# Norm, quantisation and transposes of x rearranged in a fused attention and gate kernel

## The chip, the cores and the metric

The kernel runs on one core of a Trainium2 chip. The metric is device time in microseconds of one execution. Engines: TensorE (PE, matmuls), VectorE (DVE), ScalarE (ACT), GpSimd (POOL) and SyncE (SP, which issues all DMA transfers here).

## The reference

For each of 8 batches of 512 tokens with 512 features, x is layer-normed to xn; `s` is a differential attention over xn, `g` a gate from xn and a weight that are both rounded to MXFP4; the result is `x + s * g`.

```python
qkv = hidden_states @ Wqkv_w.T + Wqkv_b            # 16 q heads, 8 k heads, 4 v of 256
p1 = attn_map(q[:, :, :, 0], k[:, :, :, 0])        # causal softmax
p2 = attn_map(q[:, :, :, 1], k[:, :, :, 1])
p = p1 - lam * p2
o = jnp.einsum('bhqk,bkhe->bqhe', p, v)
rms = jax.lax.rsqrt(jnp.mean(o * o, axis=-1, keepdims=True) + EPS)
o = o * rms * subln_w * (1.0 - LAMBDA_INIT)
s = o.reshape(B, S, H * D) @ out_w.T + out_b
# gate: blocks of 32 share a power-of-two scale; elements are rounded to e2m1
g = silu(quant_dequant_mxfp4(xn) @ quant_dequant_mxfp4(weight).T + bias)
x = x + s * g
```

## The kernel before

Every operand of a large matmul is kept as two float16 parts, high and low, and each product is three matmuls (lines 456 to 458: high by high, high by low, low by high). The high part is written by ScalarE (a scaled copy), the low one by VectorE (`scalar_tensor_tensor`: scaled value minus the high part).

A batch is 32 steps: 4 groups `g` (a pair of key heads with their values) of 8 steps. A step `r` is one query block of 128 tokens (`i = r // 2`) of one head pair, with row width `w` = 128, 256, 384 or 512 (causal). The steps of all batches are numbered through by `n`. Each engine runs its own list of instructions in order and waits on semaphores.

TensorE in step n: `scores(n + 2)` into one of two PSUM pairs, then the step's fills, then `attend(n)`. Fills are the other matmul work, put into steps by `schedule`: q, k and v projections of the next group (`PROJ`), the output projection `out` of the batch before (48 matmuls, in steps 1, 3, 5, 7), transposes of the normed x (`xT`, steps 22, 23), transposes of the quantised x (`aT`) and the gate projection (`ffn`, in steps 9, 11, 13, 15; in the last batch steps 23, 25, 27, 29). Two PSUM banks take turns as fill targets. In the last batch the output projection of its first blocks is cut into pieces (`last`).

VectorE in step n: `combine(n + 1)` (reciprocal of the second sum, coefficient, p1 + coefficient * p2 into the SBUF tile `pp`), `maxima(n + 2, 1)`, `p_lo(n + 1)`, `maxima(n + 2, 0)`, `normalised_lo(n - 1)`, evictions of fills, and between them a share of the preparation of the next x: `bn_stats` and six operations of quantisation per 128 tokens. The plan of that share is a table (`NORM_STEPS`, `QUANT_STEPS`, `PREP_AT`), over steps 9 to 31.

ScalarE in step n: `square_o(n - 1)` (sum of squares), `p_hi(n + 1)`, `normalised(n - 1)`, the two exps of `exps(n + 2)` with their sums, then fills; the last of these is the tanh of the gate into `t2`, a view of the tile `v32` that the v fills use too. It waits until GpSimd has multiplied the gate of the tanh before (`gate_done`), since that reads `t2`.

GpSimd in step n: `norm_of(n - 1)` (add, power -0.5), `gating` of the gate of step n - 1 or `finish` of an output (times gate, plus residual), root and normalisation of the next x, the rounding of the quantisation (`round_off`), the low part of v, and last `eps_of(n + 2)`, two 128x1 operations, which wait for `exps(n + 2)`.

SyncE issues the DMA transposes of the probabilities (`ph` to `pT`, needed by `attend`) and of the attention output (`on` to `oT`, tile `heads`), loads of x, residuals and the stores. A setup ahead of the first step transposes and splits all weights; the x of the first batch is normed and quantised there.

## Time and profile before

| | us |
|---|---|
| three runs | 1776.7, 1780.74, 1782.26 (median 1780.74) |
| the profiled execution | 1780.72 |
| its span, first to last instruction | 1778.5 |
| TensorE busy | 1569.9 (88%) |
| VectorE busy | 1237.2 (70%) |
| ScalarE busy | 874.0 (49%) |
| GpSimd busy | 737.3 (41%) |
| mean granted TensorE clock | 0.963 |

The profiled execution took 1780.72 us, 2.2 more than its span. Busy shares are means over stages with different limits, so the rows below cut a batch into stretches. The DMA engines' queue q1 is busy for 29.9% of the span; a transpose of the probabilities takes 2.7 us in the median from its issue to landing. The rows of a stretch (rows 2, 3 and 11) show the stretch, its length, busy us (and instructions) of PE, PEld, DVE, ACT and POOL, the granted clock as a share of full speed, the busy share of the DMA engines and GB/s; where a tile is named, those of its own engines alone. In the chain that ended last TensorE has 36%, VectorE 28%, GpSimd 13%.

### The profile page before, as it was taken

What the parts mean: (1) busy time and instruction counts of PE and PEld (TensorE: products, weight loads), DVE (VectorE), ACT (ScalarE), POOL (GpSimd) and SP (SyncE); (2) the same over time, 40 slices, a digit from 0 to 9 for tenths busy, and PEclk for the clock granted to TensorE, in tenths of its full rate; (3) what the DMA queues carried; (4) which work ended last, traced back from release to release, by engine and by line L of the source; (5) the groups of instructions that cost most, each with busy time, mean ns of one, the idle gap of its engine ahead of it and who ended that gap; (6) DMA issues with size and microseconds to landing.
All of it is one profiled execution on the core that took longest, in us unless ns stands there. A gap on an engine that the chain in (4) does not pass through costs nothing.

```text
span 1778.5 us, 29365 instructions
## 1 busy us (share of the span) xinstructions
PE 1569.9 (88%) x9425; PEld 921.1 (52%) x9425; DVE 1237.2 (70%) x3213; ACT 874.0 (49%) x2514; POOL 737.3 (41%) x1442
## 2 busy tenths in 40 slices
PE   2657898998889988999889988899988998899998
PEld 2334554555554555555554555545555555555554
DVE  4668888548884588746885488845887478854782
ACT  4554555335653356434553356534564355533561
POOL 2214563236542464324642364424643246323243
PEclk9888999999899999999999998999989999899999
DMA  7302223332233222332233223322233222322342
GB/s 266 95 1 68 49 45 63 76 61 56 55 83 61 55 50 55 81 73 50 49 59 78 66 51 57 84 57 59 47 62 75 72 50 54 54 55 65 60 77 69
DMA packets 331980, 117.55 MB, mean 66 GB/s; under 512 B 312978, under 2 KB 313524, under 8 KB 331828
## 3 DMA queue, kind: packets, MB, share of 16 engines
q1 hardware_dynamic: 331828, 115.70, 29.9%
q8 instruction: 75, 1.23, 0.3%
q14 instruction: 77, 0.63, 0.1%
HBM read 31.74 MB, written 8.39 MB: 23 GB/s over the span
## 4 chain that ended last, share of the span: by engine, by line
PE 36%; DVE 28%; POOL 13%; issue 12%; ACT 10%; DMA 1%; POOLq 0%; SPq 0%; ACTq 0%; DVEq 0%
PE ps L456 11%; PE ps L458 11%; PE ps L457 11%; DVE ps L935 5%; DVE qkv L891 4%; DVE pp L947 4%; DVE ph L953 4%; ACT qkv L635 3%; ACT ph L670 3%; DVE coef L944 2%; POOL norm L1138 2%; POOL gate L1112 2%; ACT pp L662 2%; POOL qkv L1098 2%; POOL v L1110 1%
## 5 line engine op out<-in xcount | busy, mean ns | idle before, releaser
L456 PE MATMUL ps<-xT,wqkv 128*128 128x512 f16 x768 | 297.5, 387 | 26.4 <-DVE qkv L891 24.6
L670 ACT ACTIVATE ph<-pp,small 128x128 f16<-128x128 f32 (+3 forms) x256 | 143.3, 560 | 320.3 <-DVE pp L947 319.3
L457 PE MATMUL ps<-xT,wqkv 128*128 128x512 f16 x768 | 296.1, 386 | 0.0
L458 PE MATMUL ps<-xT,wqkv 128*128 128x512 f16 x768 | 295.7, 385 | 0.0
L935 DVE CUSTOM_DVE_ANT_0 ps<-ps,mask,ssc 128x384 f32<-128x384 f32 (+3 forms) x512 | 281.9, 551 | 6.1 <-PE ps L520 6.1
L891 DVE SCALAR_TENSOR_TENSOR qkv<-ps,bsc,qkv 128x512 f16<-128x512 f32 x192 | 142.8, 747 | 140.4 <-ACT qkv L635 140.4
L674 ACT ACTIVATE junk<-ps 128x256 bf16<-128x256 f32 x256 | 97.1, 379 | 261.2 <-PE ps L458 261.1
L456 PE MATMUL ps<-qkv,pT 128*128 128x256 f16 x640 | 182.0, 284 | 37.8 <-DMA pT<-ph 36.6
L1136 POOL TENSOR_TENSOR norm<-norm,sumsq 128x1 f32<-128x1 f32 x256 | 49.5, 193 | 389.8 <-ACT junk L674 389.6
L953 DVE SCALAR_TENSOR_TENSOR ph<-pp,small,ph 128x128 f16<-128x128 f32 (+3 forms) x256 | 174.1, 680 | 43.1 <-ACT ph L670 30.6
L456 PE MATMUL ps<-wout,heads 128*128 128x512 f16 x512 | 194.1, 379 | 3.6 <-DVE small L921 3.3
L457 PE MATMUL ps<-wout,heads 128*128 128x512 f16 x512 | 194.0, 379 | 0.0
L458 PE MATMUL ps<-wout,heads 128*128 128x512 f16 x512 | 194.0, 379 | 0.0
L925 DVE SCALAR_TENSOR_TENSOR res<-ps,small,obias 128x512 f32<-128x512 f32 x32 | 24.0, 750 | 236.5 <-PE ps L458 236.5
L458 PE MATMUL ps<-qkv,pT 128*128 128x256 f16 x640 | 182.3, 285 | 0.0
L457 PE MATMUL ps<-qkv,pT 128*128 128x256 f16 x640 | 181.8, 284 | 0.0
L1128 POOL TENSOR_TENSOR norm<-psum_l 128x1 f32<-128x1 f32 x256 | 50.6, 198 | 306.9 <-ACT pp L662 306.9
L662 ACT ACTIVATE pp<-ps,ebias 128x128 f32<-128x128 f32 (+3 forms) x256 | 135.0, 527 | 85.9 <-DVE ebias L935 85.2
L1138 POOL TENSOR_TENSOR norm<-norm,small 128x1 f32<-128x1 f32 x256 | 163.9, 640 | 20.0
L518 PE MATMUL ps<-qkv 128*128 128x384 f16 (+3 forms) x512 | 153.3, 305 | 10.7 <-DVE pp L947 7.6
L456 PE MATMUL ps<-wqkv,xT 128*128 128x256 f16 x512 | 141.2, 276 | 16.8 <-DVE v L902 9.8
L519 PE MATMUL ps<-qkv 128*128 128x384 f16 (+3 forms) x512 | 153.2, 305 | 0.0
(146 smaller groups left out, 3441.9 us busy)
## 6 DMA issues: line engine op xcount, KB each, us to landing
xin<-in_L_attn_hidden_states SPq DMA_DIRECT2D x8, 1024.0 KB, 5.6
...
pT<-ph SPq DMA_TRANSPOSE x256, 2.7
heads<-on SPq DMA_TRANSPOSE x256, 2.5
...
```

The source lines that it names most:

```text
L456: mm(out, ah, bh, start=start and j == 0, stop=False)
L457: mm(out, ah, bl, start=False, stop=False)
L458: last = mm(out, al, bh, start=False, stop=stop and j == n - 1)
L518: mm(out, qh, k[:, 0, m, 0:w], start=True, stop=False)
L519: mm(out, qh, k[:, 1, m, 0:w], start=False, stop=False)
L662: run(sc if m else pp[:, 0:w], sc, ACT.Exp, bias=ebias[:, u, m:m + 1], scale=-1.0, accum_out=psum_l[:, n % 4, m:m + 1]).then_inc(exp_done, 1)
L670: run(ph[:, u, 0:w], pp[:, 0:w], ACT.Copy, scale=sigma).then_inc(ph_hi, 1)
L674: run(junk[:], o_ps[n % 2], ACT.Square, scale=SQ_SCALE, accum_out=sumsq[:, n % 2:n % 2 + 1])\
L891: stt(out=dst(kind, g, j, 1), in0=bank, scalar=bsc[:, g, c:c + 1], in1=dst(kind, g, j, 0), op0=ALU.add, op1=ALU.subtract).then_inc(fill_fr ...
L935: nc.vector.tensor_tensor_reduce(sc, sc, mask[:, S - w:S], ssc[:, c:c + 1], BIG, ALU.add, ALU.min, ebias[:, u, m:m + 1]).then_inc(max_done, 1)
L953: stt(out=ph[:, u, w:2 * w], in0=pp[:, 0:w], scalar=sigma, in1=ph[:, u, 0:w], op0=ALU.mult, op1=ALU.subtract).then_inc(ph_lo, 1)
L1138: pt(nr[:, 2:3], nr[:, 1:2], minushalf, ALU.pow).then_inc(norm_done, 1)
```

## The change

- The coefficient of a step (`-lam * l1 / l2`) is computed by GpSimd in `eps_of`, as a power of -1 and a `tensor_scalar`; `combine` is one VectorE operation that writes PSUM, and both `p_hi` and `p_lo` read it there. `scores(n + 2)` waits for `p_lo(n)` instead of `combine(n)`. On GpSimd `eps_of(n + 2)` stands right behind `norm_of(n - 1)`, ahead of gating, finishing and roundings.
- x is split into high and low before it is transposed (`x_hi` on ScalarE, `x_lo` on VectorE, steps 15, 17, 18, 19), and turned by DMA (`X_TURN`, steps 21, 22). The quantised x and the gate weight are turned by DMA as well. `xT`, `aT` and `wT` are gone from TensorE.
- Quantisation of a batch's own x is in steps 1 to 4 (`QUANT_AT`), also in the first batch, where the setup did it; the gate weight's is in steps 5 to 8 of the first batch. Statistics are all in step 7 (`NORM_AT`), and the normalisation is a ScalarE operation there.
- The gate projections are in steps 10 to 13 of every batch (`FFN_STEP`). The v fills of group 2 are in steps 15 and 16, the fills of group 3 in steps 16 to 21.
- VectorE evicts an output projection a step later, behind `p_lo` (`late`); ScalarE's square stands behind `p_hi` there.

```diff
+W_STEP = 5
+X_STEP = 5
+FFN_STEP = 10
+QUANT_AT = {(s + ds, slot): [(k + a, op) for a, op in ops] for s, k in ((1, 0), (3, 2)) for ds, slot, ops in (
+    (0, "maxima", [(0, 0), (0, 1), (0, 2), (0, 3)]),
+    (0, "projected", [(0, 4), (0, 5), (1, 0), (1, 1), (1, 2), (1, 3)]),
+    (1, "projected", [(1, 4), (1, 5)]))}
+NORM_AT = {7: range(NT)}
...
-        at = range(STEPS) if g < 3 else (0, 0, 1, 1, 2, 3, 4, 5)
+        at = (None, PROJ_AT, PROJ_AT[:6] + (7, 8), (0, 1, 1, 2, 3, 3, 4, 5))[g]
...
-        first = STEPS if has_next else LAST_STEP
-        steps[first + 2 * k].append(("aT", 0, k))
-        steps[first + 2 * k + 1].append(("ffn", 0, k))
+        steps[FFN_STEP + k].append(("ffn", 0, k))
...
+X_SPLIT = {15: 0, 17: 1, 18: 2, 19: 3}
+X_TURN = {21: (0, 1), 22: (2, 3)}
...
+                for k in X_TURN.get(s, ()) if b + 1 < B else ():
+
+                    sp.wait_ge(fill_done, fill_of("v", b, G - 1, k // 2) + 1)
+                    transpose_x((b + 1) * NT + k)
...
-                wait(pe, comb_done, n - 1)
+                wait(pe, ph_lo, n - 1)
...
+            def layer_norm(k, n):
+                act.wait_ge(centred, n + 1)
+                run(xin[:, k, :], xin[:, k, :], ACT.Identity, scale=rstd[:, n % NT, 1:2], bias=rstd[:, n % NT, 2:3])\
+                    .then_inc(xn_done, 1)
...
             def combine(n):
                 u, w = n % 2, place(n)[3]
-                l1, l2 = psum_l[:, n % 4, 0:1], psum_l[:, n % 4, 1:2]
-                dve.wait_ge(exp_done, 2 * n + 2)
-                nc.vector.reciprocal(recip[:], l2).then_inc(recip_done, 1)
-                dve.wait_ge(recip_done, n + 1)
-                stt(out=coef[:, u:u + 1], in0=recip[:], scalar=neglam, in1=l1, op0=ALU.mult, op1=ALU.mult)\
-                    .then_inc(coef_done, 1)
                 dve.wait_ge(coef_done, n + 1)
-                stt(out=pp[:, 0:w], in0=sc_ps[u][:, 1, 0:w], scalar=coef[:, u:u + 1], in1=pp[:, 0:w],
+                stt(out=sc_ps[u][:, 1, 0:w], in0=sc_ps[u][:, 1, 0:w], scalar=coef[:, u:u + 1], in1=pp[:, 0:w],
                     op0=ALU.mult, op1=ALU.add).then_inc(comb_done, 1)
...
                 pool.wait_ge(exp_done, 2 * n + 2)
-
-                wait(pool, on_lo, n - 3)
-                pt(nr[:, 0:1], l1, l1, ALU.mult).then_inc(l2_done, 1)
-                pool.wait_ge(l2_done, n + 1)
-                pt(nr[:, 3:4], nr[:, 0:1], eg[:, g:g + 1], ALU.mult).then_inc(eps_done, 1)
+                pt(recip[:], l2, minusone, ALU.pow).then_inc(recip_done, 1)
+                pool.wait_ge(recip_done, n + 1)
+                nc.gpsimd.tensor_scalar(coef[:, n % 2:n % 2 + 1], recip[:], l1, neglam, ALU.mult, ALU.mult)\
+                  .then_inc(coef_done, 1)
+
+                wait(pool, on_lo, n - 5)
+                nc.gpsimd.tensor_scalar(nr[:, 0:1], l1, l1, eg[:, g:g + 1], ALU.mult, ALU.mult).then_inc(eps_done, 1)
...
             for n in range(NSTEPS):
                 b, s = n // NS, n % NS
                 if n:
                     norm_of(n - 1)
-                    for f in PLAN[n - 1]:
-                        if f.kind == "ffn":
-                            gating(f)
...
+                if n + AHEAD < NSTEPS:
+                    eps_of(n + AHEAD)
+                for f in PLAN[n - 1] if n else ():
+                    if f.kind == "ffn":
+                        gating(f)
...
-                if n + 2 < NSTEPS:
-                    eps_of(n + 2)
```

`AHEAD` is 2, so the depth of the loop is as before.

GpSimd in the fourth batch, steps 10 and 11 (in part), before: L1136 and L1138 are `norm_of`, L1110 and L1112 `gating`, L1065 and L1068 the normalisation of the next x, L1128 and L1130 `eps_of`.

```order
L1136 TENSOR_TENSOR norm<-norm,sumsq 128x1
L1138 TENSOR_TENSOR norm<-norm,small 128x1
L1110 TENSOR_TENSOR v<-v,small 128x512
L1112 TENSOR_TENSOR gate<-v,gate 128x512
L1065 TENSOR_TENSOR xin<-xin,mv 128x512
L1068 TENSOR_TENSOR xin<-xin,rstd 128x512
L1128 TENSOR_TENSOR norm<-psum_l 128x1
L1130 TENSOR_TENSOR norm<-norm,small 128x1
```

After, the fourth batch, step 12 and the head of step 13 (L1173, L1175 are `norm_of`; L1161, L1163, L1167 `eps_of`; L1145, L1147 `gating`):

```order
L1173 TENSOR_TENSOR var<-norm,sumsq 128x1
L1175 TENSOR_TENSOR norm<-var,small 128x1
L1161 TENSOR_TENSOR recip<-psum_l,small 128x1
L1163 TENSOR_SCALAR coef<-recip,psum_l,small 128x1
L1167 TENSOR_SCALAR norm<-psum_l,small 128x1
L1145 TENSOR_TENSOR v<-v,small 128x512
L1147 TENSOR_TENSOR gate<-v,gate 128x512
L1173 TENSOR_TENSOR var<-norm,sumsq 128x1
L1175 TENSOR_TENSOR norm<-var,small 128x1
```

The gating moved from ahead of `eps_of` to behind it, and is there in steps that follow each other instead of in every second one.

ScalarE in the fourth batch, from the tanh of step 11 to the square of step 13, before: L650 is the tanh, L674 `square_o`, L670 `p_hi`, L682 `normalised`, L662 the exps, L635 a fill's copy.

```order
L650 ACTIVATE v<-gate 128x512
L674 ACTIVATE junk,sumsq<-ps 128x256
L670 ACTIVATE ph<-pp,small 128x384
L682 ACTIVATE on<-ps,norm 128x2x128
L662 ACTIVATE ps,psum_l<-ps,ebias 128x512
L662 ACTIVATE pp,psum_l<-ps,ebias 128x512
L635 ACTIVATE qkv<-ps,bsc 128x512
L674 ACTIVATE junk,sumsq<-ps 128x256
```

After, from the tanh of step 11 to the `p_hi` of step 13 (L669 is the tanh, L694 `square_o`, L690 `p_hi`, L702 `normalised`, L681 the exps, L658 a fill's copy):

```order
L669 ACTIVATE v<-gate 128x512
L694 ACTIVATE junk,sumsq<-ps 128x256
L690 ACTIVATE ph<-ps,small 128x384
L702 ACTIVATE on<-ps,norm 128x2x128
L681 ACTIVATE ps,psum_l<-ps,ebias 128x512
L681 ACTIVATE pp,psum_l<-ps,ebias 128x512
L658 ACTIVATE qkv<-ps,bsc 128x512
L669 ACTIVATE v<-gate 128x512
L694 ACTIVATE junk,sumsq<-ps 128x256
L690 ACTIVATE ph<-ps,small 128x512
```

A tanh now stands behind each pair of exps, with the next square and `p_hi` behind it.

## Rows read from the trace of the kernel before

**Rows 1.** The page, part 1: busy time of TensorE, with its share and instructions.
```profile
PE 1569.9 (88%) x9425; PEld 921.1 (52%) x9425; DVE 1237.2 (70%) x3213; ACT 874.0 (49%) x2514; POOL 737.3 (41%) x1442
```

**Rows 2.** Busy time in stretches: stages of the fifth batch (stretch, its length, engines).
```profile
939.28:1015.99 76.71, 76.71 (x423) 41.15 (x422) 36.16 (x90) 25.63 (x77) 20.78 (x43) 0.98 0.31 70
1015.99:1060.10 44.11, 39.23 (x262) 23.95 (x260) 37.10 (x99) 25.48 (x74) 27.17 (x49) 1.00 0.29 61
1060.10:1091.97 31.87, 30.89 (x194) 18.48 (x191) 26.81 (x68) 18.01 (x51) 20.91 (x37) 1.00 0.27 48
1091.97:1109.73 17.76, 13.17 (x75) 9.17 (x74) 15.77 (x42) 11.70 (x36) 5.54 (x18) 0.71 0.30 60
1109.73:1146.31 36.58, 31.47 (x210) 19.18 (x208) 31.03 (x80) 20.40 (x59) 15.90 (x32) 1.00 0.30 59
```

**Rows 3.** Stretches again: first batch, steps 1-8; last batch, steps 8-15, 16-21.
```profile
137.89:191.98 54.09, 41.30 (x251) 24.74 (x249) 43.62 (x108) 24.64 (x73) 25.21 (x42) 0.87 0.26 59
...
1637.27:1674.09 36.82, 34.19 (x230) 21.65 (x228) 27.09 (x76) 22.52 (x67) 12.20 (x33) 1.00 0.35 72
1674.09:1705.79 31.70, 30.91 (x194) 18.62 (x192) 23.74 (x63) 19.53 (x58) 9.33 (x26) 1.00 0.28 51
```

**Rows 4.** Timeline of TensorE (start, length, both us): first matmul, and behind the 48th.
```profile
1153.53 0.39 PE L456 MATMUL ps<-wout,heads 128*128 128x512 f16 x1
...
1163.89 0.27 PE L456 MATMUL ps<-qkv,pT 128*128 128x256 f16 x1
```

**Rows 5.** Timeline of VectorE, last batch, step 13.
```profile
1661.56 0.75 DVE L947 SCALAR_TENSOR_TENSOR pp<-ps,coef,pp 128x512 f32<-128x512 f32 x1
...
1663.09 0.75 DVE L953 SCALAR_TENSOR_TENSOR ph<-pp,small,ph 128x512 f16<-128x512 f32 x1
1663.76 0.75 DVE L935 CUSTOM_DVE_ANT_0 ps<-ps,mask,ssc 128x512 f32<-128x512 f32 x1
...
1666.67 0.15 DVE L942 RECIPROCAL recip<-psum_l 128x1 f32<-128x1 f32 x1
...
1667.11 0.75 DVE L947 SCALAR_TENSOR_TENSOR pp<-ps,coef,pp 128x512 f32<-128x512 f32 x1
```

**Rows 6.** Timeline of ScalarE, the same stretch.
```profile
1662.34 0.72 ACT L670 ACTIVATE ph<-pp,small 128x512 f16<-128x512 f32 x1 [1.56 <-DVE pp L947]
...
1664.61 0.69 ACT L662 ACTIVATE pp<-ps,ebias 128x512 f32<-128x512 f32 x1 [0.52 <-DVE ebias L935]
```

**Rows 7.** Timeline of the DMA queue of SyncE, the same stretch.
```profile
1663.87 1.23 SPq L395 DMA_TRANSPOSE pT<-ph  x1
```

**Rows 8.** Timeline of TensorE, the same stretch.
```profile
1667.61 0.28 PE L456 MATMUL ps<-qkv,pT 128*128 128x256 f16 x1 [1.91 <-DMA pT<-ph]
```

**Rows 9.** Timeline of GpSimd, the same stretch.
```profile
1665.46 0.19 POOL L1128 TENSOR_TENSOR norm<-psum_l 128x1 f32<-128x1 f32 x1 [3.79 <-ACT pp L662]
```

**Rows 10.** Instructions by line, whole span (busy us, mean ns of one).
```profile
L1138 POOL TENSOR_TENSOR norm<-norm,small 128x1 f32<-128x1 f32 x256 | 163.9, 640 | 20.0
...
L674 ACT ACTIVATE junk<-ps 128x256 bf16<-128x256 f32 x256 | 97.1, 379 | 261.2 <-PE ps L458 261.1
...
L1112 POOL TENSOR_TENSOR gate<-v,gate 128x512 f32<-128x512 f32 x32 | 42.9, 1339 | 2.5
...
L1110 POOL TENSOR_TENSOR v<-v,small 128x512 f32<-128x512 f32 x32 | 35.3, 1102 | 0.0
...
L871 DVE BATCH_NORM_STATS2 stats<-xin 128x6 f32<-128x512 f32 x32 | 22.0, 688 | 0.1
...
L650 ACT ACTIVATE v<-gate 128x512 f32<-128x512 f32 x32 | 20.2, 630 | 47.9 <-DVE gate L917 31.5 <-POOL qkv L1098 16.4
```

**Rows 11.** Stretch of the first batch, instructions on the tile am alone (quantisation).
```profile
137.89:191.98 54.09, 12.20 (x21) 0.87 0.26 59
```

**Rows 12.** Timeline of VectorE, the fifth batch, beside a v low part on GpSimd.
```profile
1096.41 1.21 DVE L944 SCALAR_TENSOR_TENSOR coef<-recip,small,psum_l 128x1 f32<-128x1 f32 x1
```

**Rows 13.** Timeline of VectorE in the setup.
```profile
94.46 0.69 DVE L773 SCALAR_TENSOR_TENSOR xres<-am,xres 128x512 f32<-128x512 f32 x1 [6.13 <-POOL xres L1055]
```

More of the change, by code:

```diff
@@ L164, in setup_order @@
 def setup_order():
-    order = [("w", n) for n in range(8)] + [("fill", i) for i in range(NT)]
-    i = NT
+    order = [("w", n) for n in range(8)]
+    i = 0
     for n in range(8, WB):
@@ L555, in _ @@
                     pe.wait_ge(fill_free, len(PROLOGUE) - 2)
-                    scores(1)
+                    for a in range(1, AHEAD):
+                        scores(a)
                     continue
@@ L1022, in _ @@
+                if n + AHEAD < NSTEPS and not late:
+                    maxima(n + AHEAD, 1)
+                if n + AHEAD - 1 < NSTEPS:
+                    p_lo(n + AHEAD - 1)
+                for f in late:
+                    fill(f)
+                if n + AHEAD < NSTEPS:
+                    if late:
+                        maxima(n + AHEAD, 1)
+                    maxima(n + AHEAD, 0)
+                prepare(b, s, "maxima")
                 if n:
                     normalised_lo(n - 1)
-                prepare_some(b, s, 1)
```

421 lines of the change are left out of this document (218 added, 203 removed).

## The prediction

> **What bounds the kernel now.** I read the page first: TensorE is busy 1569.9 of 1778.5 us [rows 1], so at most some 200 us can be won without taking matmuls away. Then I cut one ordinary batch (the fifth, 207.0 us in all) into stages of its 32 steps and asked for each engine's busy time in them [rows 2]. Steps 0 to 7 take 76.71 us with TensorE busy for all of it. Steps 8 to 15: 44.11 with 39.23 busy. Steps 16 to 21: 31.87 with 30.89. Steps 22 to 24: 17.76 with 13.17, at a mean granted clock of 0.71, so for part of it at the lower of its two levels, 1.2 instead of 2.4 GHz. Steps 25 to 31: 36.58 with 31.47. So in the first quarter only fewer matmuls would help, and in the rest the loop over VectorE, ScalarE and GpSimd decides in part.
>
> How much matmul work a step has follows from the spacing: 48 matmuls of 512 columns from 1153.53 to 1163.89 are 0.216 us each [rows 4]. A q, k or v fill is 12 times 512 columns (v 24 times 256), 2.60 us; an output projection 10.4; a gate projection 0.87; scores plus attend 0.97, 1.62, 2.27, 1.62 in the four pairs of steps of a group. That makes 180.0 us a batch, and 4.3 more for the transposes of x and of the quantised x (16 float32 blocks of four passes, 16 bf16 ones).
>
> The loop that TensorE waits for can be followed in the last batch, which prepares no next x [rows 5, 6]: combine starts at 1661.56, the high part 1662.34, the low part 1663.09, the second maximum 1663.76, the second exp 1664.61, then fill copy and fill eviction, the reciprocal at 1666.67, the coefficient, and the next combine at 1667.11: 5.55 us round, against 4.9 to 5.2 us of matmuls. The transpose of the result is issued at 1663.87 and the attend starts at 1667.61 [rows 7, 8], 6.05 us after its combine. I call the end of the second exp of a step X.
>
> **The change, part by part.**
>
> *Transposes leave TensorE.* 4.3 us less work a batch. They sat in steps 8 to 15 (aT, 0.87) and 22, 23 (xT, 3.46). What is late there next is worked out below.
>
> *Coefficient on GpSimd.* Today GpSimd begins at 1665.46, 0.16 us behind X (1664.61 + 0.69) [rows 6, 9]. The new chain there is a power (0.64 on average, 0.55 where nothing disturbs it), then a tensor_scalar, 1.05 us from X to a usable coefficient if the tensor_scalar costs what a 128x1 operation does (0.20). The trace has no tensor_scalar on GpSimd; its ends are 0.19 and the power's 0.64 [rows 9, 10], and I take 0.20, the like shape. In a step with a fill the copy and eviction take 1.37 us from X (to 1666.67), so the coefficient is hidden and VectorE saves 0.45 us between eviction and combine (1666.67 to 1667.11): 5.55 becomes 5.1. At 0.64 it would be about even with today.
>
> *The low part reads PSUM.* An SBUF-only VectorE operation is held up by GpSimd: the 0.22 us coefficient took 1.21 us at 1096.41, beside the low part of v on GpSimd, a 128x512 operation [rows 12]. The low part had the same two SBUF operands. The Trainium skill has a rule for it (SBUF — State Buffer, "Who interferes with whom"): a VectorE instruction with two SBUF inputs contends with a GpSimd one that reads SBUF, one with a single SBUF input does not. By that rule the low part is now free of it, and the new quantisation operations, two SBUF inputs each, are exposed beside GpSimd's finishing and rounding: that is the second rival. The sum below does not use the rule.
>
> *Quantisation and statistics into steps 1 to 4 and 7.* In an ordinary batch an output projection of 10.4 us stands in each of steps 1, 3, 5, 7. In step 1 come 1.7 us to the second maximum, 2.0 for four operations, 2.6 for GpSimd's rounding (two 128x512 operations [rows 10]), 1.3 for two more and 2.1 for four of the next tensor; in step 2 about 8.2, since GpSimd's norm stands behind the second rounding. That is 17.9 us for steps 1, 2 and, with wider rows, 19.4 for 3, 4, against 18.2 and 19.5 us of matmuls: just hidden, cost 0. If not, the excess is there in all seven batches. The late output eviction lies in the same covered steps: 0.
>
> *Steps 25 to 31* lose the quantisation. Matmuls 30.2 us; what is left is the loop at 5.1 against 4.9 in two steps and the wait for the last transposes, about 1.5: 31.7 instead of 36.6, **-4.9**.
>
> *Steps 22 to 24.* Matmuls are now 1.62, 1.62, 3.57, so the loop decides. From the start of step 21 the combines for 22 and 23 come at about +1.2 and +6.2, attend 22 ends at 8.1, attend 23 at 13.1. x blocks 2 and 3 are issued behind the transpose of step 23, at 1.2 us each, and land 3.3 to 3.7 us later [rows 7, 8]: +14.2, the moment TensorE has done the scores. Step 24 ends at 17.1, less 4.87 for step 21 is 12.3. TensorE idles as much there as today, and today the clock falls there [rows 2], which doubles the two attends: 14.5 instead of 17.8, **-3.3**.
>
> *Steps 8 to 15, the loss.* The gate projections now stand in four steps running (10 to 13), and GpSimd handles the gate of a step only behind the coefficient of the step two ahead. ScalarE's tanh writes the tile that GpSimd's gating of the one before still reads, and behind that tanh stand the square, then the high part of the next step. From X: coefficient and epsilon 1.33, gating 1.10 + 1.34, tanh 0.63, square with its sum 0.55 [rows 10], high part 0.75, low part 0.67, maximum to exp 0.85, exp 0.69: 8.0 us for the next X at 512 columns, 7.7 and 7.3 for the neighbours. Three such rounds are 23.0 us, where TensorE has 5.1, 5.7, 5.7. Followed through from step 8: X of 10 at 3.9, of 13 at 21.0, then 28.7, 36.7, 44.0. Scores 17 wait for the low part of 15 (43), the v fill and attend 15 (transposed 3.5 later) end at 47.7. So 47.7 instead of 44.1, **+3.6**, though 3.5 us of matmuls (aT 0.9 and one v fill) have left the stage.
>
> *Steps 16 to 21* have that v fill: 33.1 us of matmuls, plus 1.7 for the lag and the two fills in one step, 34.8 instead of 31.9: **+2.9**.
>
> *Clock.* In steps 14 and 15 TensorE would idle about half the time, more than in steps 22 to 24 today, behind which the clock fell [rows 2]. Between 0 and 4 us a batch; I take **+1.0**.
>
> An ordinary batch: -4.9 - 3.3 + 3.6 + 2.9 + 1.0 = -0.7. Seven times (the first batch from step 9 counts as one): **-4.9**.
>
> *Setup.* VectorE waits there 6.13 us for a rounding that GpSimd puts behind its all-reduce [rows 13]; it and the operations of the quantisation are gone. Against it the scales of group 0 come about 4 us later (four copies of x stand before four squares on ScalarE) but lose two roundings in the chain. **-10** (bounds -14 and 0).
>
> *First batch, steps 1 to 8.* No output projection covers them, and they now hold eight quantisations instead of four. Today 54.09 us, TensorE busy 41.30 [rows 3], and four quantisations put 12.20 us on VectorE (all but the first operation of each) [rows 11]. After: steps 1, 2: 17.9; 3, 4: 19.4. Steps 5 to 8 carry a weight block each: 3 us to the second maximum, 2.0 for four operations, GpSimd's rounding 2.6, two more 1.3: 9.2, 8.8, 11.6 (with four statistics of 0.69 and what follows each [rows 10]), 10.2. Sum 77, less 1 for overlap at the ends: **+22** (bounds 12 and 30).
>
> *Last batch.* Its steps 8 to 15 took 36.82 us [rows 3], because its gates came later, from step 22 on. Now they take 47.7 there: +10.9. Steps 16 to 21: 31.70 to 34.8, +3.1. Clock +1.0. From step 22 on the gates are gone (-3.5 to -4.3 of matmuls), but the loop decides in most of those steps: -2.5. **+12.5**.
>
> The profiled execution's own time is 1780.72 us, the median of the runs 1780.74. 1780.7 - 4.9 - 10 + 22 + 12.5 = **1800 us**.
>
> **The rivals.**
>
> *The tanh does not queue.* If gating finds enough room (the v fill and scores behind it hide the rounds), steps 8 to 15 need about 41 us, as today's 4.9 us of idle beside 34.6 us of matmuls and a little. Then a batch is -0.7 - 6.7 = -7.4, seven are -52, the last +5.8 and setup and first batch +12: 1747 us, faster. For it: today's four gates, in alternate steps, leave TensorE 4.9 us idle in the stage, about 1.2 each [rows 2]. Against it: the rounds above are sums of measured durations in an order that the semaphores force. It decides if a round is under 6 us.
>
> *The x quantisation is not hidden.* The margin in steps 1 to 4 is under half a us. The new operations with two SBUF inputs may be held up by GpSimd as the coefficient was, 1.0 us each [rows 12]. With two such stalls in each pair, 4 us in each of six batches: 1824, slower still.
>
> *GpSimd's tensor_scalar costs 0.64.* Then epsilon ends 0.9 later, in every uncovered step that the loop decides, some 12 a batch at 0.4: 5 us, in eight batches 40: 1840.
>
> *The gains and losses cancel.* Clock 0, first batch +15, last +9, setup -12 and a batch at -2: 1779, no change.
>
> **How the numbers follow.** Slower by the sum (with its costlier forms) 0.60; tanh not queuing, or each step's loss at its lower bound, 0.29; cancelling 0.11. What a measurement of this kernel tells from no change is about 0.3%, 5 us. Faster 0.29, the same 0.11, slower 0.60. The range from 1750 to 1838 reaches nearly to the two outer cases; the likeliest case alone would have 1784 to 1824.
>
> **What would show it.** Steps 10 to 14 of each batch show ScalarE's tanh waiting for GpSimd's gate product, with some 8 us from one second exp to the next, and TensorE waiting in steps 13 to 15. Steps 0 to 7 stay at 76 us. Steps 1 to 8 of the first batch take over 70 us. Steps 25 to 31 fall to 32 us. If the tanh waits for nothing there, the forecast is wrong at its main step; if steps 25 to 31 don't fall, the coefficient chain is dearer than 1.05 us.

## The result: 1.4% faster, where slower was forecast

The changed kernel took 1755.57 us (median of 4 runs, 1753.57 to 1758.27), the kernel before 1781.08 (4 runs, 1776.70 to 1782.26). The ratio is 0.9862, with a 95% interval of 0.9838 to 0.9886. The forecast was 1800: the sign was wrong, and the time lies in the lower part of the stated range, 1750 to 1838. The profiled execution took 1753.57 us, with a span of 1751.8. One of the six runs of the version with GpSimd's old order, further down, took 2711.73 us at a granted clock of 0.555 and is left out of its figures.

The page first, the row that answers to [rows 1]:

```profile
PE 1533.0 (88%) x9137; PEld 898.6 (51%) x9153; DVE 1092.5 (62%) x2665; ACT 888.2 (51%) x2542; POOL 882.3 (50%) x1673
```

VectorE lost 145 us of work and GpSimd gained 145. The stages of the fifth batch after the change, in the order of [rows 2] (steps 0 to 7, 8 to 15, 16 to 21, 22 to 24, 25 to 31):

```profile
926.90:1002.19 75.29, 75.29 (x423) 40.56 (x421) 48.10 (x111) 28.26 (x78) 43.77 (x72) 1.00 0.29 71
1002.19:1048.51 46.32, 38.49 (x221) 21.94 (x220) 26.30 (x65) 24.34 (x72) 25.74 (x47) 0.93 0.36 69
1048.51:1081.69 33.18, 33.18 (x219) 21.15 (x216) 25.23 (x57) 22.75 (x62) 16.14 (x33) 1.00 0.26 48
1081.69:1094.91 13.22, 7.53 (x59) 4.94 (x57) 6.75 (x22) 7.33 (x28) 7.66 (x18) 1.00 0.80 151
1094.91:1126.20 31.29, 30.46 (x210) 19.67 (x208) 23.05 (x57) 21.04 (x63) 13.84 (x36) 1.00 0.41 73
```

The batch takes 199.3 us instead of 207.0: -1.4, +2.2, +1.3, -4.5, -5.3. The means of the six ordinary batches (the second to the seventh) are 199.2 and 207.0: -0.8, +1.5, +1.4, -4.1, -5.8, so the fifth is ordinary in sum, less so in its stages. Steps 1 to 8 of the first batch, the next two steps, and steps 8 to 15 of the last batch [rows 3], and then the stretch of [rows 11], VectorE's work on the tile am in those first steps:

```profile
132.31:194.92 62.61, 40.05 (x230) 23.00 (x227) 45.85 (x104) 21.28 (x64) 36.05 (x50) 0.89 0.26 54
194.92:221.78 26.86, 10.52 (x50) 5.21 (x50) 17.37 (x46) 12.03 (x32) 15.44 (x32) 0.81 0.23 39
...
1601.46:1648.00 46.54, 37.52 (x225) 21.30 (x225) 26.02 (x65) 24.51 (x73) 25.74 (x47) 0.96 0.39 69
```

```profile
132.31:194.92 62.61, 21.30 (x40) 0.89 0.26 54
```

The kernel before, in steps 9 and 10 of its first batch, and then TensorE in step 9 after the change:

```profile
191.98:201.39 9.41, 9.05 (x55) 4.94 (x53) 8.50 (x25) 5.64 (x18) 3.62 (x10) 1.00 0.14 28
```

```profile
206.67 0.39 PE L545 MATMUL ps<-qkv 128*128 128x256 f16 x1 [11.58 <-DVE ph L982]
```

Over the whole program: setup to the end of step 0 -5.6 us, the rest of the first batch +17.0, six ordinary batches -46.8, the last batch +8.7. That is -26.7, the difference of the two spans. The first batch's +17.0 is +8.5 in steps 1 to 8, +17.5 in steps 9 and 10, where TensorE waits 11.58 us for a low part, and -9.0 from step 11 on.

The tanh queue is there as forecast. GpSimd, then ScalarE, in step 12 of the fifth batch (start, length, both us):

```profile
1021.00 0.55 POOL L1161 TENSOR_TENSOR recip<-psum_l,small 128x1 f32<-128x1 f32 x1 [1.71 <-ACT pp L681]
1021.65 0.34 POOL L1163 TENSOR_SCALAR coef<-recip,psum_l,small 128x1 f32<-128x1 f32 x1
1021.97 0.34 POOL L1167 TENSOR_SCALAR norm<-psum_l,small 128x1 f32<-128x1 f32 x1
1022.27 1.04 POOL L1145 TENSOR_TENSOR v<-v,small 128x512 f32<-128x512 f32 x1
1023.39 1.26 POOL L1147 TENSOR_TENSOR gate<-v,gate 128x512 f32<-128x512 f32 x1
```

```profile
1020.25 0.58 ACT L681 ACTIVATE pp<-ps,ebias 128x384 f32<-128x384 f32 x1
...
1020.81 0.69 ACT L658 ACTIVATE qkv<-ps,bsc 128x512 f16<-128x512 f32 x1
1024.73 0.63 ACT L669 ACTIVATE v<-gate 128x512 f32<-128x512 f32 x1 [3.23 <-issue]
```

GpSimd sat waiting for the exp (1.71 us), did the coefficient, and only then the gate product (to 1024.65). The next tanh starts 0.08 us behind it, after 3.23 us of idle time; the row says "issue", that is, the profile names no releaser, but in the program the tanh waits for that product (`gate_done`), and the first two experiments bear it out. This happens three times a batch; second exps end at 1020.83, 1028.38, 1036.07 and 1043.05, rounds of 7.55, 7.69 and 6.98 us where 7.7, 8.0 and 7.3 were forecast.

### The profile page after: what moved, and what is told of

Read it like the earlier page. It is cut to its first block and busy times, and to the rows that moved or that the text cites. A ratio compares the mean times of both kernels' runs of the same rounds, so it can differ in the third digit from the quotient of the medians.

```text
span 1751.8 us, 28271 instructions
## 1 busy us (share of the span) xinstructions
PE 1533.0 (88%) x9137; PEld 898.6 (51%) x9153; DVE 1092.5 (62%) x2665; ACT 888.2 (51%) x2542; POOL 882.3 (50%) x1673
## 5 line engine op out<-in xcount | busy, mean ns | idle before, releaser
L1161 POOL TENSOR_TENSOR recip<-psum_l,small 128x1 f32<-128x1 f32 x256 | 140.3, 548 | 482.4 <-ACT pp L681 482.4
L490 PE MATMUL ps<-xT,wqkv 128*128 128x512 f16 x768 | 296.7, 386 | 20.3 <-DVE qkv L940 18.5
L690 ACT ACTIVATE ph<-ps,small 128x128 f16<-128x128 f32 (+3 forms) x256 | 134.4, 525 | 349.6 <-DVE ps L976 349.0
L970 DVE CUSTOM_DVE_ANT_0 ps<-ps,mask,ssc 128x384 f32<-128x384 f32 (+3 forms) x512 | 279.6, 551 | 18.8 <-PE ps L547 18.5
L982 DVE SCALAR_TENSOR_TENSOR ph<-ps,small,ph 128x128 f16<-128x128 f32 (+3 forms) x256 | 141.0, 551 | 117.1 <-ACT ph L690 108.7
L702 ACT ACTIVATE on<-ps,norm 128x256 f16<-128x256 f32 x256 | 120.6, 471 | 169.4 <-POOL norm L1175 165.5
L545 PE MATMUL ps<-qkv 128*128 128x384 f16 (+3 forms) x512 | 154.1, 307 | 55.9 <-DVE ph L982 53.5
L976 DVE SCALAR_TENSOR_TENSOR ps<-ps,coef,pp 128x128 f32<-128x128 f32 (+3 forms) x256 | 141.4, 552 | 68.2 <-POOL coef L1163 67.9
L988 DVE SCALAR_TENSOR_TENSOR on<-ps,norm,on 128x256 f16<-128x256 f32 x256 | 123.2, 481 | 94.1 <-ACT on L702 91.4
L546 PE MATMUL ps<-qkv 128*128 128x384 f16 (+3 forms) x512 | 154.3, 307 | 0.0
L547 PE MATMUL ps<-qkv 128*128 128x384 f16 (+3 forms) x512 | 154.3, 307 | 0.0
L1175 POOL TENSOR_TENSOR norm<-var,small 128x1 f32<-128x1 f32 x256 | 142.7, 557 | 20.1
L681 ACT ACTIVATE pp<-ps,ebias 128x128 f32<-128x128 f32 (+3 forms) x256 | 134.8, 527 | 29.6 <-DVE ebias L970 28.5
```

Of the source, the lines that this page charges most:

```text
L490: mm(out, ah, bh, start=start and j == 0, stop=False)
L545: mm(out, qh, k[:, 0, m, 0:w], start=True, stop=False)
L546: mm(out, qh, k[:, 1, m, 0:w], start=False, stop=False)
L547: last = mm(out, ql, k[:, 0, m, 0:w], start=False, stop=True)
L970: nc.vector.tensor_tensor_reduce(sc, sc, mask[:, S - w:S], ssc[:, c:c + 1], BIG, ALU.add, ALU.min, ebias[:, u, m:m + 1]).then_inc(max_done, 1)
L976: stt(out=sc_ps[u][:, 1, 0:w], in0=sc_ps[u][:, 1, 0:w], scalar=coef[:, u:u + 1], in1=pp[:, 0:w], op0=ALU.mult, op1=ALU.add).then_inc(comb_ ...
```

## The experiments

All were timed in five rounds beside the kernel before, and ratios are to it. Its own median was 1781.1 us beside the changed kernel and 1774.8 to 1778.0 beside the others, so a difference in us between two rows of the table is uncertain by up to some 6 us; where it matters the ratios' answer stands beside it. The table has the stages of the fifth batch, cut as above (us), the batch, the median and the ratio with its interval; the experiments follow it.

| kernel | 0-7 | 8-15 | 16-21 | 22-24 | 25-31 | batch | median | ratio (95%) |
|---|---|---|---|---|---|---|---|---|
| before | 76.7 | 44.1 | 31.9 | 17.8 | 36.6 | 207.0 | 1781.1 | 1 |
| after | 75.3 | 46.3 | 33.2 | 13.2 | 31.3 | 199.3 | 1755.6 | 0.986 (0.984-0.989) |
| after, gating first | 75.3 | 39.3 | 33.2 | 13.6 | 31.4 | 192.7 | 1707.1 | 0.960 (0.959-0.962) |
| after, gating on VectorE | 75.3 | 39.4 | 33.2 | 13.7 | 31.7 | 193.3 | 1705.5 | 0.959 (0.957-0.961) |
| after, coefficient on VectorE | 75.3 | 43.3 | 33.2 | 14.2 | 34.5 | 200.5 | 1752.5 | 0.986 (0.984-0.987) |
| after, low part from SBUF | 75.4 | 45.0 | 33.9 | 13.8 | 30.3 | 198.3 | 1754.4 | 0.987 (0.986-0.988) |
| after, output evicted early | 79.9 | 52.7 | 33.2 | 14.8 | 31.1 | 211.6 | 1821.3 | 1.026 (1.025-1.028) |
| after, x not quantised | 75.3 | 45.3 | 33.3 | 13.7 | 31.0 | 198.5 | 1753.7 | 0.988 (0.986-0.990) |
| after, GpSimd's old order | 79.4 | 39.5 | 33.2 | 17.4 | 31.0 | 200.5 | 1760.9 | 0.991 (0.989-0.993) |
| before, x not quantised | 75.9 | 43.7 | 30.6 | 15.7 | 33.6 | 199.3 | 1731.6 | 0.974 (0.972-0.976) |
| before, x turned twice | 75.7 | 44.1 | 31.9 | 17.7 | 37.2 | 206.6 | 1783.9 | 1.005 (1.003-1.006) |
| before, x not normalised | 75.6 | 43.3 | 31.7 | 17.6 | 36.6 | 204.8 | 1765.2 | 0.994 (0.993-0.996) |
| before, new order of GpSimd | 77.8 | 50.7 | 33.3 | 19.8 | 37.5 | 219.1 | 1876.1 | 1.055 (1.054-1.057) |
| before, coefficient on GpSimd | 77.6 | 45.7 | 34.5 | 19.7 | 34.2 | 211.6 | 1818.1 | 1.023 (1.021-1.025) |
| before, both of these | 78.7 | 55.1 | 33.9 | 21.8 | 35.8 | 225.2 | 1927.1 | 1.084 (1.083-1.086) |

**Gating first (the queue's price).**

```
+  for f in PLAN[n - 1] if n else ():
+      if f.kind == "ffn":
+          gating(f)
   if n + AHEAD < NSTEPS:
       eps_of(n + AHEAD)
   ... (the gating that stood behind it is gone)
```

> The changed kernel with one order turned round on GpSimd: gating of the gate projection before stands ahead of the reciprocal, coefficient and epsilon of the step two ahead. Changed kernel: 1755.6 us, 0.986 of before. Queue theory (tanh waits for gating, gating waits behind the coefficient chain; measured rounds of 7.55, 7.69 and 6.98 us between second exps 13 to 16 of the fifth batch): gating then runs while VectorE and ScalarE work towards the next exp, tanh waits for nothing, rounds fall to 5.5 to 6 us, steps 8 to 15 from 46.3 to 42 to 43.5 us a batch, eight batches: 1725 to 1735 us, ratio 0.970 to 0.975. Rival (TensorE is held there by something else, the narrow attends and the v fill, and the tanh waits in time that is spare): under 5 us, 1750 to 1756, ratio 0.984 to 0.986. Rival two (gating now delays the coefficient by up to 2.4 us instead): stage unchanged or longer, 1756 to 1765.

Measured 1707.12 us, faster than the 1725 to 1735 of the queue theory and far from both rivals: the theory holds, and the queue was worth more than I gave it. The rounds between second exps fall from 7.55, 7.69 and 6.98 us to 5.74, 5.88 and 5.17. GpSimd in the same step:

```profile
995.56 1.04 POOL L1145 TENSOR_TENSOR v<-v,small 128x512 f32<-128x512 f32 x1
996.68 1.27 POOL L1147 TENSOR_TENSOR gate<-v,gate 128x512 f32<-128x512 f32 x1
997.90 0.55 POOL L1161 TENSOR_TENSOR recip<-psum_l,small 128x1 f32<-128x1 f32 x1
```

```profile
996.55 0.58 ACT L681 ACTIVATE pp<-ps,ebias 128x384 f32<-128x384 f32 x1
...
999.22 0.63 ACT L669 ACTIVATE v<-gate 128x512 f32<-128x512 f32 x1 [1.42 <-DVE gate L952]
```

The gate product lies in the time in which GpSimd used to wait for the exp. It ends just behind it, so the coefficient starts 0.77 us after the second exp (997.13) where it started 0.17 after it (1020.83), and the tanh waits for its own eviction alone. Steps 8 to 15 fall from 46.32 to 39.31 (in the mean of six batches from 45.6 to 40.0):

```profile
978.46:1017.77 39.31, 35.53 (x222) 20.56 (x220) 26.10 (x65) 24.14 (x70) 25.69 (x47) 1.00 0.41 80
```

**Gating on VectorE.** One `(t2 + 1) * gate` behind the second maximum, GpSimd's two operations gone; finish waits for it.

```
-  pt(t2, t2, one.broadcast_to([P, HID]), ALU.add)
-  pt(gate[:, f.j, :], t2, gate[:, f.j, :], ALU.mult).then_inc(gate_done, 1)
+  stt(out=gate[:, f.j, :], in0=t2, scalar=1.0, in1=gate[:, f.j, :], op0=ALU.add, op1=ALU.mult)
```

> The changed kernel with gating as one VectorE operation, (tanh + 1) times gate, behind the second maximum, instead of two GpSimd operations of 1.10 and 1.34 us. Queue theory: the queue goes altogether, at about 0.65 us of VectorE in four steps of a batch: rounds of 5.7 to 6.2 us, steps 8 to 15 at 42 to 43.5, 1725 to 1735 us (0.970 to 0.975), as with gating first. Rival (tanh waits in spare time): 1753 to 1760. Between the two: if VectorE is the engine of those rounds, this one comes out 3 to 8 us slower than gating first on GpSimd.

Measured 1705.53: two ways to take the queue away give the same time, so it is the queue that cost 48 to 50 us, or 46 to 48 by the ratios.

**Before, x not quantised.** Leaves out the quantisation of each x but the first.

```
 for k, op in prep_share(s, slot) if b + 1 < B else ():
+    if op == PREP - 1:
+        nc.vector.tensor_copy(aq[:, k, :], xin[:, k, :]).then_inc(q_done, 1)
+    if op > 1: continue
```

> The kernel before, with the quantisation of every x but the first left out (its four operations behind the statistics on VectorE and the two of GpSimd's rounding; a plain copy writes the tile). Theory that the quantisation moved out of steps 12 to 31 gives the change its gain: steps 25 to 31 of the fifth batch fall from 36.58 to 31.3 to 32.5 us, steps 0 to 7 by 1.4, steps 22 to 24 by 1 to 2; a batch from 207.0 to 198 to 200, seven of them: 1725 to 1735 us, ratio 0.969 to 0.975. Rival (the coefficient on GpSimd and the low part from PSUM shorten every loop, and the quantisation was mostly covered): steps 25 to 31 stay above 34.5, a batch above 204, 1760 to 1775 us.

Measured 1731.56, as the theory had it, with a fifth batch of 199.3: 7.7 us less, as much as the whole change gives (mean of six batches 200.0, 7.0 less). But steps 25 to 31 fell by 3.0 only, not by the expected 4 to 5; the rest of that stage's gain is another part's.

**After, x not quantised.** The same left out of the changed kernel.

> The changed kernel (1755.6 us) with the quantisation of every x but the first left out (a plain copy writes the tile). Theory (in steps 1 to 4 it lies wholly beside the output projections, as TensorE's waits there of 0.0 us say): unchanged, 1752 to 1758 us, ratio 0.984 to 0.988. Rival (it delays something that comes due later, the gate transposes or the first loop steps 9 to 11): 1 to 2 us less a batch, 1740 to 1749 us.

Measured 1753.65, as the theory had it: in steps 1 to 4 the quantisation costs next to nothing (0.4 us in the mean of six batches). The two together show the move worth about 7 us a batch.

**Output evicted early.** The one part whose worth I had not looked for.

```
-  late = [f for f in PLAN[n - 1] if f.kind == "out"] if n else []
+  late = []
```

and the like on ScalarE, so that the square stands ahead of the high part again.

> The changed kernel (1755.6 us) with the late output eviction undone: the projection's result is evicted in its own step, behind the low part of the step before, and the square stands ahead of the high part again. Prediction's term (the late eviction lies in covered steps and is worth 0): steps 0 to 7 of the fifth batch stay at 75 us, 1752 to 1759 us, ratio 0.984 to 0.988. Rival (VectorE now waits out the 10.4 us projection with the second half of the quantisation behind it, so the quantisation no longer fits): the excess is 3 to 8 us in steps 1 to 4 of each batch but the first, 1775 to 1810 us.

Measured 1821.28: 66 us slower than the changed kernel (72 by the ratios), beyond even the rival. VectorE, then ScalarE, at the end of step 1:

```profile
967.97 0.73 DVE L940 SCALAR_TENSOR_TENSOR qkv<-ps,bsc,qkv 128x512 f16<-128x512 f32 x1
975.38 0.75 DVE L960 SCALAR_TENSOR_TENSOR res<-ps,small,obias 128x512 f32<-128x512 f32 x1 [6.68 <-PE ps L492]
```

```profile
975.70 0.38 ACT L694 ACTIVATE junk<-ps 128x256 bf16<-128x256 f32 x1 [8.92 <-PE ps L492]
```

VectorE waits out 6.68 us of the projection and ScalarE 8.92, with the second half of the quantisation behind the eviction. Step 3 becomes 2.8 us longer and step 5 1.7, and step 9 takes 10.2 us instead of 3.6:

```profile
1045.22 0.40 PE L545 MATMUL ps<-qkv 128*128 128x256 f16 x1 [3.63 <-DVE ph L982]
```

That wait is there in each of the six ordinary batches. The low part waits for the high one, which stands on ScalarE behind the four normalisations of step 7 (1039.69 to 1044.16); they follow VectorE's four statistics, and these start only when the eviction is done (1037.41). The rest of the longer step is matmuls at a granted clock of 0.67. That the quantisation is hidden only because eviction and square are late follows from steps 3 and 5, but it wasn't tried without the quantisation, and which of the two does more wasn't tried either.

**Coefficient on VectorE.**

> The changed kernel (1755.6 us) with the softmax coefficient back on VectorE, a reciprocal and a 128x1 operation of 0.22 us in front of combine; GpSimd keeps the epsilon alone. Theory of the prediction (0.45 us on the loop in each step that the loop decides, some 8 to 12 a batch, against a coefficient chain of 1.15 us that the fill's eviction hides): steps 22 to 24 and 30, 31 of the fifth batch longer by 2 to 3 us together; but in steps 12 to 15 the gating starts 0.9 us sooner behind the second exp, so the rounds of 7.5 us shrink to about 6.7, 2 to 3 us back. Net 0 to +1.5 a batch: 1752 to 1768 us, ratio 0.984 to 0.993. Rival (the coefficient's move carries the gain of 7.8 us a batch): 1790 us or more.

Its edit takes the power and the tensor_scalar out of `eps_of` and puts the reciprocal and the 128x1 operation ahead of combine, as the kernel before has them. Measured 1752.45, the same as the changed kernel. Both halves of the expectation show: steps 25 to 31 are 3.2 us longer, steps 8 to 15 3.0 shorter, since gating starts sooner (the batch is 0.9 longer in the mean of six, and the last batch 5.6 shorter):

```profile
1004.81:1048.12 43.31, 38.09 (x221) 22.12 (x220) 31.43 (x79) 24.77 (x74) 20.09 (x34) 0.92 0.39 74
1095.53:1130.05 34.52, 31.16 (x210) 19.29 (x207) 26.23 (x74) 21.46 (x64) 8.68 (x22) 1.00 0.39 64
```

**Low part from SBUF.** Combine writes `pp`, high and low part read it, the second exp waits for the low part.

> The changed kernel with combine writing the SBUF tile pp again, high and low part reading it, scores waiting for combine and the second exp for the low part. Theory (the low part reads PSUM only to be free of GpSimd): the low part goes from 0.55 back to 0.68 us on average, and some of that lies in loop-decided steps: 0 to +1 us a batch, 1753 to 1765 us, ratio 0.985 to 0.991. Rival (the SBUF operands let GpSimd hold VectorE up in the steps with gating and rounding, 1 us each time): +3 us a batch or more, over 1775 us.

Measured 1754.44, the same. The low part (mean of 256, the changed kernel first, then this one):

```profile
L982 DVE SCALAR_TENSOR_TENSOR ph<-ps,small,ph 128x128 f16<-128x128 f32 (+3 forms) x256 | 141.0, 551 | 117.1 <-ACT ph L690 108.7
```

```profile
L982 DVE SCALAR_TENSOR_TENSOR ph<-pp,small,ph 128x128 f16<-128x128 f32 (+3 forms) x256 | 157.5, 615 | 123.3 <-ACT ph L690 111.9
```

The mean is 64 ns higher with two SBUF operands, but only through the instructions that run beside wide work of GpSimd. With no 128x512 instruction of GpSimd beside it the low part takes 0.35, 0.48, 0.62 or 0.75 us by its width in both kernels; beside one, the 128x128 form stays at 0.35 in the changed kernel and takes 0.63 in the mean here (31 cases each). One of them, beside a low part of v that GpSimd runs from 931.92 to 933.07:

```profile
932.50 0.72 DVE L982 SCALAR_TENSOR_TENSOR ph<-pp,small,ph 128x128 f16<-128x128 f32 x1
```

The Trainium skill (SBUF — State Buffer, "Who interferes with whom") says that a VectorE instruction with two SBUF inputs contends with a GpSimd one that reads SBUF; the trace agrees. The 16 us of busy time more moved nothing.

**Before, new order of GpSimd, coefficient on GpSimd, and both.** The change lets GpSimd's `eps_of` stand right behind the norm, ahead of gating, finish, rounding and the low part of v; before, it stood last in the step.

```
 norm_of(n - 1)
+if n + 2 < NSTEPS:
+    eps_of(n + 2)
 ... gating, finish, normalise, round_off, v_low
-if n + 2 < NSTEPS:
-    eps_of(n + 2)
```

> The kernel before (1780.7 us) with one part of the change alone: the coefficient on GpSimd as a power and a tensor_scalar, with the epsilon behind them, ahead of gating, finish and rounding, right behind the norm. Theory (0.45 us in loop-decided steps, but these steps hold GpSimd's rounding of 2.6 us, behind which the coefficient now stands): between -1.5 and +1.5 us a batch, 1768 to 1792 us, ratio 0.993 to 1.006. Rival (this part carries the gain): 1730 to 1755 us. Rival (it needs the quantisation moved away first, since the coefficient queues behind the rounding): over 1792 us.

Both together measured 1927.13, 149 us slower than the kernel before beside it (1777.96), the last of the three cases and far past its bound, so I asked which part it was.

> The kernel before (1780.7 us) with GpSimd's order alone changed as the change has it: the epsilon of the step two ahead right behind the norm, ahead of gating, finish, normalisation, rounding and the low part of v. The coefficient stays on VectorE. With both, the time was 1927 us, 147 more. Theory (the order does it: GpSimd waits for the second exp first and then does 2.4 to 2.7 us of wide work that used to fill that wait, and the next norm, behind which ScalarE's next exps stand, comes after it): 1860 to 1927 us, ratio 1.045 to 1.085. Rival (the coefficient itself is what comes late): 1781 to 1795 us.

> The kernel before with the coefficient on GpSimd, but GpSimd's order as it was: coefficient and epsilon last in the step, behind the wide operations. Theory (the order does it): the wide work ends before the second exp in most steps, so the coefficient is late only in a few: 1775 to 1800 us, ratio 0.997 to 1.011. Rival (a coefficient on GpSimd is late whatever the order, while GpSimd has wide work in the loop's steps): over 1850 us.

The order alone: 1876.08 (+5.5%, 98 us), as the theory had it. The coefficient alone, in the old order: 1818.08 (+2.3%, 40 us), between the two cases, so a coefficient on GpSimd is late there in more steps than the theory allowed. GpSimd in step 11, before and with the new order alone:

```profile
1028.05 1.04 POOL L1110 TENSOR_TENSOR v<-v,small 128x512 f32<-128x512 f32 x1
1029.17 1.27 POOL L1112 TENSOR_TENSOR gate<-v,gate 128x512 f32<-128x512 f32 x1
1030.39 1.04 POOL L1065 TENSOR_TENSOR xin<-xin,mv 128x512 f32<-128x512 f32 x1
1031.58 1.06 POOL L1068 TENSOR_TENSOR xin<-xin,rstd 128x512 f32<-128x512 f32 x1
...
1033.02 0.19 POOL L1136 TENSOR_TENSOR norm<-norm,sumsq 128x1 f32<-128x1 f32 x1
```

```profile
1085.72 0.19 POOL L1128 TENSOR_TENSOR norm<-psum_l 128x1 f32<-128x1 f32 x1 [1.71 <-ACT pp L662]
...
1086.13 1.04 POOL L1110 TENSOR_TENSOR v<-v,small 128x512 f32<-128x512 f32 x1
...
1090.65 0.50 POOL L1136 TENSOR_TENSOR norm<-norm,sumsq 128x1 f32<-128x1 f32 x1
```

The second exp of the step starts at 1029.05 and 1084.97. Before, the wide work begins 1.00 us ahead of it; in the new order 1.16 behind, and the norm, for which ScalarE's next exps stand in line, follows the exp by 5.68 us instead of 3.97.

**GpSimd's old order in the changed kernel.** `eps_of` last in the step.

> The changed kernel with GpSimd's coefficient and epsilon last in every step, behind gating, finish, rounding, low part of v and the roots, the order of the kernel before. Gating ahead of them alone gave 1707 us. Theory (wide work belongs ahead of the wait): gating gains as before; v's low part no longer stands behind the wait either: 1695 to 1710 us, ratio 0.953 to 0.962. Rival (in steps 1 to 4 the rounding, which itself waits for VectorE, now holds the coefficient back by several us there, beside a covered stretch with under 1 us to spare): 1715 to 1750 us.

Measured 1760.9, the rival's mechanism and dearer than its 1715 to 1750. Steps 8 to 15 gain all that gating first gave, but the coefficient now stands behind the rounding, which waits for VectorE, and behind the work of steps 22 to 24. VectorE waits for it 2.88, 3.67 and 3.68 us in steps 1, 2 and 4; the second of these:

```profile
952.26 0.49 DVE L976 SCALAR_TENSOR_TENSOR ps<-ps,coef,pp 128x256 f32<-128x256 f32 x1 [3.67 <-POOL coef L1163]
```

The stages 0 to 7, 8 to 15 and 22 to 24:

```profile
930.45:1009.85 79.40, 75.98 (x423) 40.26 (x421) 46.32 (x114) 29.34 (x83) 43.33 (x72) 1.00 0.28 68
1009.85:1049.36 39.51, 36.68 (x223) 21.93 (x221) 26.71 (x66) 25.27 (x74) 25.59 (x47) 0.96 0.43 81
1082.54:1099.97 17.43, 10.47 (x60) 6.42 (x59) 8.33 (x26) 8.67 (x31) 7.73 (x19) 0.71 0.63 121
```

Neither order is right for all work: what is ready belongs ahead of the wait, what itself waits behind it.

**Before, x turned twice.** The blocks of x are transposed twice in steps 22 and 23.

> The kernel before (1780.7 us) with the float32 transposes of x on TensorE done twice in steps 22 and 23 of each batch but the last: 16 more, 3.46 us of matmul work a batch. Theory (they stand on the path there, so taking them away gave the change about 3 us a batch in steps 22 to 24): +3 to +3.5 us in each of seven batches, 1802 to 1806 us, ratio 1.012 to 1.014. Rival (TensorE idles 7 us in these steps and the transposes hide in it; the gain of 4.6 us there came from the quantisation or the loop): +0 to +1 us a batch, 1781 to 1788 us.

Measured 1783.92 against 1774.79 beside it, ratio 1.0045 (1.0031 to 1.0060), the rival's case, and in the fifth batch steps 22 to 24 are no longer than in [rows 2]:

```profile
1089.72:1107.45 17.73, 12.52 (x91) 9.20 (x90) 15.76 (x42) 11.58 (x36) 5.51 (x18) 0.90 0.31 60
```

In the other six batches they take 17.7 to 18.5, as before (17.7 to 18.9), so the 9 us between the medians lie elsewhere, and no stage shows them: the profile of the kernel before, at 1780.72 us, is itself slower than the 1774.79 of this comparison. TensorE's own transposes were hidden there: doubling their 3.46 us moved the stage by nothing, and taking them away could hardly give the 4.5 that it gained.

**Before, x not normalised.** GpSimd's two wide operations on x cut to one column.

> The kernel before (1780.7 us) with GpSimd's two 128x512 operations on x in steps 10, 13, 16 and 19 cut to one column each, so x is not normalised. Theory (they stand in front of nothing that the loop needs, since the coefficient is on VectorE, and the loss that the coefficient on GpSimd brought by itself comes from standing behind them): 0 to -1 us a batch, 1773 to 1781 us, ratio 0.996 to 1. Rival (they delay gating and the low part of v and so hold steps 11 to 17, 6.5 us of waits a batch): -3 us a batch or more, under 1760 us.

Measured 1765.23 us (0.9942): 2.2 us in the fifth batch, 1.8 in the mean of six, between the cases. So these operations stood in front of something, and what was not followed.

**The first batch.** The first x is quantised in the setup on VectorE alone, the gate weight in steps 1, 3, 5, 7.

```
-W_STEP = 5
+W_AT = (1, 3, 5, 7)
...
```

> The changed kernel with the first batch's quantisations spread out again: the four x blocks are quantised in the setup, wholly on VectorE (rounding too), among the weight fills 12 to 24, and the four blocks of the gate weight stand in steps 1, 3, 5, 7 instead of 5 to 8. Theory (eight quantisations in steps 1 to 8 and four in a row before the gate projections cost what the first batch lost, 181.5 to 198.6 us): first batch back to 182 to 186, setup 132.3 to 137 to 143 since VectorE has room there: 1745 us, 1741 to 1750, ratio 0.977 to 0.983. Rival (VectorE bounds the setup, 4.6 us a block): setup +15 to +19, nothing won, 1754 to 1760.

Measured 1742.36 (0.9794, 0.9776 to 0.9813), as the theory had it: setup to the end of step 0 132.3 to 139.3, the rest of the first batch 198.6 to 178.5. In steps 9 and 10 TensorE still idles, so the eight quantisations are not the whole of the loss there:

```profile
139.32:188.13 48.81, 38.74 (x230) 22.91 (x227) 34.91 (x84) 21.89 (x64) 27.25 (x45) 0.90 0.37 75
188.13:209.33 21.20, 11.35 (x51) 5.61 (x50) 13.64 (x38) 11.81 (x31) 10.64 (x27) 0.76 0.21 44
```

**Versions put together.** First gating first with `PROJ_AT[:6] + (7, 8)` replaced by `PROJ_AT`, so that the v fills of group 2 stand in steps 14 and 15:

> The version with gating ahead of the coefficient (1707.1 us), with the v fills of group 2 back in steps 14 and 15 instead of 15 and 16. TensorE waits there 1.5 us in step 14 and 0.5 to 3 us in step 15. Theory (the v fill of 2.6 us fills an idle stretch that nothing else needs): 2 to 3 us less a batch, steps 16 to 21 fall by 2.6 us and steps 8 to 15 grow by under 1: 1685 to 1692 us, ratio 0.948 to 0.952. Rival (the loop decides steps 14 and 15 and each fill's eviction and copies, 1.4 us of VectorE and ScalarE, go onto it): 0 to 1 us a batch, 1700 to 1707 us.

Measured 1701.14 (0.9577, 0.9561 to 0.9592): 6 us, or 4 by the ratios, about 1 a batch. That is the rival's case and not the theory's 1685 to 1692. Then with the first batch's changes too:

> A version put together: gating ahead of the coefficient on GpSimd (1707.1 us alone), v fills of group 2 in steps 14 and 15 (1701.1 with it), the first batch's x quantised in the setup and the weight in steps 1, 3, 5, 7 (13 us less alone), and the first batch's four statistics and normalisations in steps 2, 4, 6, 8 instead of all in step 7, with x loaded in step 0. Theory (the 12 us that TensorE waits in step 9 of the first batch are the four normalisations behind the last weight block): step 9 falls from 16 to 5 us, steps 2 to 8 grow by 1 us each in four of them: 1701 - 13 - 7 = 1681 us, 1676 to 1686, ratio 0.943 to 0.948. Rival (the wait is the weight block's and stays): 1688 or more.

> The same version with gating as one VectorE operation instead of two GpSimd ones ahead of the coefficient. Alone the two differed by 1.6 us for VectorE, within their intervals. Expected 1676 to 1685 us, within 3 us of the other; if VectorE decides in steps 14 and 15 once the v fills stand there, 3 to 6 us slower than the other.

Measured 1692.34 (0.9529, 0.9516 to 0.9543) and 1684.96 (0.9490, 0.9477 to 0.9503). The second is the fastest kernel here, 5.1% under before. The expectation of 1681 was too low, and the first of the two lies in its rival's range (1688 or more): spreading the normalisations took the first batch from 178.5 us to 175.2, 3 us and not 7, since step 9 fell to 9.8 and not to 5. The VectorE form is 7 us faster than the GpSimd one, further apart than the 3 expected; step 17 is 7.2 us instead of 8.1 in seven batches, and why is open.

## Why the forecast was wrong

**The queue was right, and so was its price.** Forecast: with the queue steps 8 to 15 take 47.7, without it 41, so 6.7 us a batch. Measured: 46.3 and 39.3, so 7.0 (45.6 and 40.0 in the mean of six batches, so 5.7; the fifth has the largest difference). The rival "the tanh does not queue" falls, though its time, 1747, was closer.

**The failed step is the sum of an ordinary batch, -0.7 where -7.8 was measured.** Every term came out on the dear side (fifth batch):

| term | forecast | measured | what was wrong |
|---|---|---|---|
| steps 0 to 7 | 0 | -1.4 | TensorE was busy for all of the 76.7, but at a granted clock of 0.98, its lower level for 3.4 us from 938.64 on; after the change it is 1.00 (75.3). The forecast had nothing for a clock given back |
| steps 8 to 15 | +3.6 | +2.2 | second exp 13 came 18.6 us into the stage, not 21.0, the rounds were 0.8 shorter in sum |
| steps 16 to 21 | +2.9 | +1.3 | 1.7 us of lag added to matmuls that run without a gap: 33.18 busy of 33.18 |
| steps 22 to 24 | -3.3 | -4.5 | two attends were doubled for a low clock; it was 1.00 in this batch, in the other ordinary ones 0.77 to 0.88 (13.8 to 15.0 us) |
| steps 25 to 31 | -4.9 | -5.3 | |
| clock | +1.0 | 0 | what the clock cost (0.93 in steps 8 to 15) is inside the stages above |

The errors are 1.4, 1.4, 1.6, 1.2, 0.4 and 1.0, together 7.0. Over the six ordinary batches -46.8 us was measured where the sum had -4.2: 42.6 of the 46.3 us by which the sum of the changes (+19.6) missed the difference of the spans (-26.7), and the sign. The lag was counted twice, at the end of steps 8 to 15 and again in the next stage.

**The other terms.** Setup -5.6 instead of -10; the first batch +17.0 instead of +22 less an ordinary batch's 0.7; the last +8.7 instead of +12.5. That the first batch comes out near is luck. Steps 1 to 8 take 62.6 us where the forecast had over 70, so +8.5 and not +22, and steps 9 and 10, for which it had nothing, take 17.5 more. There TensorE waits 11.58 us for a low part whose high part stands on ScalarE behind four normalisations, and these behind the last weight block's quantisation. Spreading the quantisations takes 20.1 us out of this batch and puts 7.0 into the setup; spreading the normalisations too brings step 9 from 16.1 to 9.8 us.

**Where the gain came from.** Leaving the quantisation out gives the kernel before 7.7 us in the fifth batch and the changed one 0.8, so its move is worth about 7 (6.6 in the mean of six), nearly as much as the whole batch gained. The rest of the change gives some 7 more (gating first: 192.7) less the queue's 7.0. In steps 25 to 31 it gives 3.0 of 5.3; the coefficient's place is worth 3.2 there, given back in steps 8 to 15. My -4.9 there was nearly right as a sum, not in its parts. In steps 22 to 24 it gives 2.0 of 4.5, the coefficient 1.0, the transposes' matmuls nothing measurable. The remaining 1.5 may be the copies and evictions of the transposed x, which left ScalarE and VectorE; that was not tried alone. So where the other 7 us a batch come from is open in part: undoing the coefficient's move, or the low part's source, changed the whole kernel by nothing clear of noise, and the late eviction was undone only together with the quantisation in its new place.

**What the forecast priced at nothing.** The late eviction "lies in the same covered steps: 0". With it the steps are covered, as forecast; without it the changed kernel is 2.6% slower than the one before. And no rival asked where GpSimd's wide work stands against its wait, though the queue was that very thing.
